# Two attention blocks and two expert layers on one core: last two pairs of batches with banks of their own, three context tiles ahead

## The reference, cut to what matters

```python
x = x + tanh(g_xattn[0]) * L0_xattn(layernorm(x), ctx, ctx)          # 32 batches x 128 rows x 256, 16 heads
x = x + tanh(g_ffn[0])   * L0_ffn(layernorm(x))                      # 8 experts, best 2 per row, width 1024
x = x + tanh(g_xattn[1]) * L1_xattn(layernorm(x), ctx, ctx, bias)    # "second attention"
x = x + tanh(g_ffn[1])   * L1_ffn(layernorm(x))                      # 16 slots read x, one expert each; x reads the slots
```

## Time and profile before

| | |
|---|---|
| median of 3 runs | 1308.04 us (1307.53 to 1308.72) |
| the profiled execution | 1310.88 us |
| its span, first to last instruction | 1309.1 us |
| busy: PE, DVE, ACT, POOL | 1268.9, 881.8, 795.5, 747.3 us |
| mean granted clock of TensorE | 0.996 |
| second attention begins | about 757 us |
| `combine()` begins | about 1240 us |

### The profile page before, as it was taken

One profiled execution on the slowest core, in us unless ns is written; L12 is line 12 of the kernel. 1 busy time (PEld: TensorE's weight loads), 2 busy tenths in 40 slices (PEclk: granted clock), 3 DMA queues, 4 the chain that ended last, 5 costly groups with the idle time before them and its releaser, 6 DMA issues.

```text
span 1309.1 us, 38203 instructions
## 1 busy us (share of the span) xinstructions
PE 1268.9 (97%) x14755; PEld 1133.8 (87%) x14755; DVE 881.8 (67%) x2364; ACT 795.5 (61%) x1739; POOL 747.3 (57%) x835
## 2 busy tenths in 40 slices
PE   9999999998999999999999988999999999999897
PEld 8898888886999999999999967899999998655576
DVE  5888888876566556655564048999999997321386
ACT  5676676654777777777775436665566665423453
POOL 2578888754877787777773054566666643000131
PEclk9999999999999999999999989999999999999999
DMA  6675565633777777777767512621111111599712
GB/s 225 231 257 175 193 207 172 218 131 117 258 221 221 239 216 225 217 231 231 220 213 278 232 45 66 229 93 51 53 51 55 53 61 66 223 428 426 296 64 68
DMA packets 103891, 237.51 MB, mean 181 GB/s; under 512 B 8992, under 2 KB 86176, under 8 KB 91296
## 3 DMA queue, kind: packets, MB, share of 16 engines
q1 hardware_dynamic: 97568, 218.29, 48.7%
q0 software_dynamic: 6144, 16.79, 4.0%
HBM read 174.22 MB, written 60.82 MB: 180 GB/s over the span
## 4 chain that ended last, share of the span: by engine, by line
PE 89%; DVE 4%; DMA 3%; issue 2%; ACT 1%; POOL 1%; DVEq 0%; ACTq 0%; SPq 0%; PEldq 0%; POOLq 0%
PE ps L2140 14%; PE psT L2125 7%; PE ps L714 6%; PE psS L691 5%; PE ps L1084 5%; PE psT L700 4%; PE ps L1026 4%; PE ps L2125 4%; PE psS L2125 4%; PE ps L1009 2%; PE ps L1043 2%; PE ps L953 2%; PE psT L706 2%; DMA arena<-wset_dram 2%; PE ps L2381 2%
## 5 line engine op out<-in xcount | busy, mean ns | idle before, releaser
L2093 POOL TENSOR_TENSOR wb_lo<-arena,wb_hi 128x2048 fp32r<-128x2048 f32 x64 | 296.7, 4637 | 92.0 <-ACT wb_hi L2216 92.0
L2140 PE MATMUL ps<-wb_hi,hT_hi 128*128 128x256 f32 x528 | 151.7, 287 | 0.0
L700 PE MATMUL psT<-arena 32*128 32x128 f32 x2048 | 149.4, 283 | 0.4 <-ACT arena L1256 0.4
L2140 PE MATMUL ps<-wb_lo,hT_hi 128*128 128x256 f32 x528 | 147.7, 280 | 0.0
L2140 PE MATMUL ps<-wb_hi,hT_lo 128*128 128x256 f32 x528 | 147.6, 280 | 0.0
L691 PE MATMUL psS<-arena 32*128 32x256 f32 x1024 | 139.7, 389 | 0.8 <-ACT arena L1333 0.4
L2216 ACT CAST wb_hi<-arena 128x1024 fp32r<-128x1024 f32 x128 | 130.7, 1045 | 4.5 <-DMA arena<-w_dram 4.3
L700 PEld LDWEIGHTS psT<-arena 32*128 32x128 f32 x2048 | 124.6, 186 | 1.7 <-issue 1.2
L1700 POOL TENSOR_TENSOR arena<-arena,eps_sb 128x1 f32<-128x1 f32 x94 | 23.7, 252 | 149.7 <-DVE arena L1571 106.5
L2281 DVE TENSOR_TENSOR arena<-ps,arena 128x512 f32<-128x512 f32 (+1 forms) x39 | 25.4, 651 | 121.5 <-PE ps L2140 81.1
L1713 POOL DMA_INDIRECT arena<-xs_rows,slot_i x64 | 64.4, 1007 | 69.3 <-DMA xs_rows<-arena 54.3
(11 more groups left out here) (508 smaller groups left out, 3862.4 us busy)
## 6 DMA issues: line engine op xcount, KB each, us to landing
arena<-wset_dram SPq DMA_DIRECT2D x24, 2048.0 KB, 16.0
xs_rows<-arena SPq DMA_DIRECT2D x33, 1024.0 KB, 8.8
arena<-w_dram SPq DMA_DIRECT2D x32, 1028.0 KB, 5.9
arena<-w_dram SPq DMA_DIRECT2D x32, 1024.0 KB, 5.9
arena<-w_dram SPq DMA_DIRECT2D x7, 2052.0 KB, 13.3
w_sb<-xs_rows SPq DMA_DIRECT2D x33, 256.0 KB, 2.7
xs_rows<-arena SPq DMA_DIRECT2D x33, 256.0 KB, 5.5
arena<-ctxT_dram SPq DMA_DIRECT2D x63, 128.0 KB, 4.3
```

The source lines that it names most:

```text
L700: nc.tensor.matmul(psT[:, b, j * P:(j + 1) * P], kbd_[p, (k - 1) % NK, c, par, :], qT[p, (k - 1) % 3, c, :], start=j == 0, stop=False, ski ...
L2093: nc.gpsimd.tensor_tensor(wb_lo[:, u % 2, part], wb_raw[:, u % 2, part], wb_hi[:, u % 2, part], ALU.subtract).then_inc(w_g.sem, 1)
L2140: last = nc.tensor.matmul(ps[5][:, t * D:(t + 1) * D], hp[:, f, t * P:(t + 1) * P], wp[:, f, :], start=f == 0 and t == 0 and n == 0, stop= ...
```

## The change

Second attention: `LATE` is 3, so that tile 10 too has its keys and values made at the entry. Its keys come right behind those of tiles 8 and 9, its values in step 0 between the transposition of tile 1 and the second half of the scores of tile 0; the bank is `ps[4]`. The eight constant products at the entry become two, with two more in step -1 and two at the head of step 0; the eight in step 0 become three. The casts of `o1`, `v1` and `dv` move ahead of the early tiles on ScalarE, the one of `dv` behind a wait for the experts' last rows on DVE. GpSimd's subtractions of `o1` and `dv` move ahead of its wait for these rows in DRAM and thus ahead of the first gather; that of `v1` moves to step 1, behind the gather of tile 4. Weight sets 0 to 2 load at steps 5 to 7 as before, set 3 at step 11 instead of 8.

`combine()`: the output products of pair 14 go to `ps[3]` and no longer wait for the residual sum of pair 13. Pair 15 is done by batches: `pn` in two halves, transpositions into `ps[2]` and `ps[5]`, two copies, output products into `ps[4]` and `ps[6]`, two residual sums, and each batch's output DMA waits for its own sum. Three constant products stand in the last step between the transpositions of pair 14 and its output products.

```diff
-LATE = 2
+LATE = 3
...
-        hi_a, lo_g = track("hi_a", "k0 v0 o1 v1 dv", 1), track("lo_g", "k0 v0 o1 v1 dv", 1)
+        hi_a, lo_g = track("hi_a", "k0 v0 o1 v1 dv", 1), track("lo_g", "k0 v0 o1 dv v1", 1)
...
-                    if not A and k == 4 + EARLY_SETS:
+                    if not A and 5 <= k < 4 + EARLY_SETS:
+                        sp.dma_start(set_at(k - 5).rearrange("p e f -> p (e f)"), a["wset"][k - 5]).then_inc(ld_set[k - 5], 16)
+                    if not A and k == ctx_first:
                         sp.wait_ge(kv_a.sem, kv_a.at(ctx_first - 1, "V"))
-                    if not A and 5 <= k < 5 + EARLY_SETS:
-                        sp.dma_start(set_at(k - 5).rearrange("p e f -> p (e f)"), a["wset"][k - 5]).then_inc(ld_set[k - 5], 16)
+                        sp.dma_start(set_at(EARLY_SETS - 1).rearrange("p e f -> p (e f)"), a["wset"][EARLY_SETS - 1])\
+                            .then_inc(ld_set[EARLY_SETS - 1], 16)
...
+                def constant_products(n, bank):
+                    for _ in range(n):
+                        nc.tensor.matmul(ps[bank][:, :], ident_b[:, :], ident_b[:, None, :].to_broadcast([P, 4, P]),
+                                         start=True, stop=True)
...
-                    for _ in range(8):
-                        nc.tensor.matmul(ps[4][:, :], ident_b[:, :], ident_b[:, None, :].to_broadcast([P, 4, P]),
-                                         start=True, stop=True)
+                    for n in range(LATE - 1):
+                        late_keys(n)
+                        late_values(n)
+                    late_keys(LATE - 1)
+                    constant_products(2, 0)
                 for k in steps:
                     if not A and k == 0:
-                        pe.wait_ge(stash_a, STASH + LATE)
+                        constant_products(2, 7)
+                        pe.wait_ge(stash_a, STASH + LATE - 1)
...
+                    if not A and k == -1:
+                        constant_products(2, 0)
+                    if not A and k == 0:
+                        late_values(LATE - 1)
                     scores(k, 1)
...
                     if not A and k == 0:
-                        for _ in range(8):
-                            nc.tensor.matmul(ps[4][:, :], ident_b[:, :], ident_b[:, None, :].to_broadcast([P, 4, P]),
-                                             start=True, stop=True)
+                        constant_products(3, 7)
...
                     nc.scalar.activation(table[:, :], ones[:, 0:1], ACT.Exp)
+                    for name in parts:
+                        if name == "dv":
+                            act.wait_ge(m0_last["y"].sem, m0_last["y"].at(UNITS - 1, "y"))
+                        nc.scalar.copy(split[name][0][:, :, :], w[name]).then_inc(hi_a.sem, 1)
...
-                    for name in parts:
-                        nc.scalar.copy(split[name][0][:, :, :], w[name]).then_inc(hi_a.sem, 1)
+                    for n in range(LATE - 1):
+                        late_away(n)
...
+                    if not A and k == 0:
+                        late_away(LATE - 1)
...
                 if not A:
+                    rest_of("o1")
+                    rest_of("dv")
                     for u in range(2):
                         pool.wait_ge(m0_last["ys"][u], 16 * ((UNITS + 1 - u) // 2))
                     gather(0)
...
+                    if not A and k == 1:
+                        pool.wait_ge(kv_p.sem, kv_p.at(early - 1, "V"))
+                        pool.wait_ge(stash_p, STASH + LATE)
+                        rest_of("v1")
...
+            last_turned, last_out = (ps[2], ps[5]), (ps[4], ps[6])
+
+            def out_bank(i):
+                return ps[3] if i == N - 2 else ps[7]
...
-                    sp.wait_ge(o_v.sem, o_v.at(i, "out"))
                     for b in range(2):
+                        sp.wait_ge(o_v.sem, o_v.at(i, "out") + (b if i == N - 1 else 0))
...
+                def last_pair():
+                    for b in range(2):
+                        pe.wait_ge(p_v.sem, p_v.at(N - 1, "pn") + b)
...
+                    for b in range(2):
+                        pe.wait_ge(t_a.sem, t_a.at(N - 1, "pT") + b)
...
+                    if i == N - 1:
+                        pe.wait_ge(v_a.sem, v_a.at(N // 2 - 1, "v3"))
+                        for _ in range(3):
+                            nc.tensor.matmul(ps[5][:, :], ident_b[:, :], ident_b[:, None, :].to_broadcast([P, 4, P]),
+                                             start=True, stop=True)
...
-                        before(pe, o_v.sem, o_v.at(i - 2, "out"))
+                        if i - 1 < N - 2:
+                            before(pe, o_v.sem, o_v.at(i - 2, "out"))
...
+                        if i == N - 1:
+                            for b in range(2):
+                                nc.vector.tensor_tensor(cpn[:, b].rearrange("p (h s) -> p h s", h=H),
+                                                        e[:, b].rearrange("p (h s) -> p h s", h=H),
+                                                        csm[:, b, :, None].to_broadcast([P, H, NS]), ALU.mult).then_inc(p_v.sem, 1)
```

More of the change, by code:

```diff
@@ L299, in build @@
         stash += [late_rows[:, n * 2 * D:(n + 1) * 2 * D] for n in range(LATE)]
-        late_ctx = [pT[:, 0, n * C * P:(n + 1) * C * P].rearrange("p (c t) -> p c t", c=C) for n in range(LATE)]
-        late_bank = (1, 2)
+        late_ctx = [pT[:, n // 2, n % 2 * C * P:(n % 2 + 1) * C * P].rearrange("p (c t) -> p c t", c=C) for n in range(LATE)]
+        late_bank = (1, 2, 4)
         dead = w_sb[:, 0:8].rearrange("p n c d -> p (n c d)")
@@ L785, in ahead_values, with late_keys, late_values @@
                     last.then_inc(stash_p, 1)
+                def late_keys(n):
+                    pe.wait_ge(ld_stash[n], 32)
+                    for m in range(C):
+                        for c in range(C):
+                            nc.tensor.matmul(ps[late_bank[n]][:, m * P:(m + 1) * P], wk[:, c, m * P:(m + 1) * P],
+                                             late_ctx[n][:, c, :], start=c == 0, stop=c == C - 1)
+                def late_values(n):
+                    for c in range(C):
+                        last = nc.tensor.matmul(ps[late_bank[n]][:, D:2 * D], late_ctx[n][:, c, :], wv[:, c, :],
+                                                start=c == 0, stop=c == C - 1)
+                    last.then_inc(stash_p, 1)
+                def constant_products(n, bank):
+                    for _ in range(n):
+                        nc.tensor.matmul(ps[bank][:, :], ident_b[:, :], ident_b[:, None, :].to_broadcast([P, 4, P]),
+                                         start=True, stop=True)
                 def last_tiles(pe):
@@ L1218, in put_away, with late_away @@
                     nc.scalar.copy(stash[stash_order[n]], ps[stash_bank[n]][:, :]).then_inc(stash_a, 1)
+                def late_away(n):
+                    act.wait_ge(stash_p, STASH + n + 1)
+                    nc.scalar.copy(stash[STASH + n], ps[late_bank[n]][:, :]).then_inc(stash_a, 1)
                 if A:
@@ L1228, in scalar @@
                         values(i, early_bank[i])
-                    for n in range(LATE):
-                        act.wait_ge(stash_p, STASH + n + 1)
-                        nc.scalar.copy(stash[STASH + n], ps[late_bank[n]][:, :]).then_inc(stash_a, 1)
-                    for name in parts:
-                        nc.scalar.copy(split[name][0][:, :, :], w[name]).then_inc(hi_a.sem, 1)
+                    for n in range(LATE - 1):
+                        late_away(n)
                 for k in steps:
@@ L2616, in tensor @@
                 for i in range(N + 1):
+                    if i == N:
+                        last_pair()
+                        break
                     if ok(i - 1):
```

55 lines of the change are left out of this document (36 added, 19 removed).

## The result

| | before | after |
|---|---|---|
| median of 6 runs each | 1308.38 us (1306.98 to 1309.13) | 1300.79 us (1298.48 to 1302.00) |
| ratio | | 0.9937, interval 0.9918 to 0.9955 |
| the profiled execution, its span | 1310.88, 1309.1 us | 1301.76, 1300.0 us |
| experts' last sum to the end of the span | 554.65 us | 543.75 us |

The change makes the kernel 7.6 us faster; forecast were 5.6. In a later and larger measurement (12 runs of the changed kernel, 32 of the one before) it was 5.7 us, ratio 0.9955 (0.9942 to 0.9968). The two intervals overlap.

The account below looks back on a forecast made before the run. TensorE, busy 97% of the span, and its low clock were taken to bound the kernel. Terms 0.75 + 1.4 - 0.1 + 0.5 + 3.1 = 5.65 us off 1308.04 gave 1302.4 us, its own range 1301.2 to 1304.6.

Parts of the forecast that it names:

- Entry: Entry of second attention: line 1072 of tile 0 starts at about 773.35 instead of 777.10, 3.75 us against the profiled execution.
- Most timed runs don't have the first fall: Clock fall at 770.2 us, entry of second attention, worth 3.0 us: taken as absent from most timed runs.
- the 0.75: Gain in us at the entry of second attention in an execution whose clock does not fall there.
- They may well have the second: Clock fall at 1299.3 us, in the last two pairs: timed runs may have it, so 3.1 us was summed there.
- The subtractions: Casts of line 1617 in steps 1 and 2 without GpSimd's subtractions beside them: 0.86 and 0.55, together 1.4 us (0 to 1.7).
- Late first gather: Subtractions of `o1` and `dv` ahead of the first gather make it later: 0.1 us loss, 1.3 as the bad end.
- Tile 10: Stream of tiles: one step less that computes its own keys and values, 0.5 us (0 to 0.6).
- The end: Last two pairs: 3.1 us gain (2.4 to 3.4) against the profiled execution, 1.6 us where the clock does not fall there.
- (b): Gathers, layer norm and GpSimd set the path into tile 1, entry gain is waited away: 1305.4 or 1306.2 us; chance 0.13.
- (d): The change does not do what it says, another wait ends last, entry gives 0.75 or less: 1307.0 us; chance 0.06.
- (a): Timed runs have both clock falls, as the profile has: gain 8.65 us, 1299.4 us; chance 0.20.
- (c): Slower: clock falls and stays down, three constant products being too few; 1311.9 us with 35 us of low clock; chance 0.06.

Follow-up runs that it names:

- before_three: The kernel before with three constant products in step 0 instead of eight, nothing else: 1306.86 us, ratio 0.9994.
- subs_in_steps: The changed kernel with GpSimd's three subtractions back in steps 0, 1 and 2: 1303.28 us, ratio 0.9973.
- before_again: The kernel before once more, unaltered, for a second trace of it: 1306.33 us, ratio 0.9988.
- late_two: The changed kernel with two tiles made early instead of three, constant products in the place of tile 10: 1302.41 us, ratio 0.9965.
- no_fill: The changed kernel without the constant products at the entry, at the head of steps -1 and 0, and in step 0: 1302.69 us, ratio 0.9980.

## Why the prediction was right or wrong

The number, 1302.4, is 1.6 us above the median; the range held it. Forecast rightly was the direction and, term by term against the profiled execution, most of the sum. The step that failed is the reading of the 2.84 us between profile and median: which of the two low stretches the timed runs have. It failed twice, in opposite directions, and the forecast gain of 5.65 us agrees with the 5.7 of the larger measurement by luck.

- **What bounds.** TensorE's own list and its low clock: right.
- **Entry, against the profile shown: 3.75 forecast, 3.94 measured.** Line 1087 comes 16.14 us after the first gather (forecast 16.4, before 20.1) and 3.3 us after the start of the second half's score products; the 3.7 that the prediction gave for this was slipped, its own 773.35 - 770.12 is 3.2. Of the measured gain 1.64 us are the longer low stretch of that one execution, 1.16 the five products less, and 1.08 the subtraction of `o1` (`before_three`, `subs_in_steps`). These three leave 0.06. The last was taken at 0.2, since in the profile it overlapped little of the cast; where it overlaps it costs over 1.
- **"Most timed runs don't have the first fall": wrong.** With it fails the 0.75. All four traces with the old entry have a fall there, and none of 117 executions has a mean clock of 1.0. Between the profile shown and `before_again` it was not the presence of that fall that differed but its length (1.64), and beside it the fall at the end (1.69) and slower steps between tiles 1 and 9 (1.48): the 5.0 us, with 0.2 later on. The median lies between the two, since other executions have low stretches in other places. In the usual execution the entry is worth 21.01 - 18.71 = 2.30 us, where the forecast had 0.75.
- **"They may well have the second": wrong too.** Of the four traces with the old end one, the profile shown, loses time to a fall there; in the three others it takes 9.35 or 9.36 us from the end of pair 14's copy to the end of the span, against 11.03. So the 3.1 in the sum should have been the 1.6 that the prediction kept for the other case. This error of 1.5 us cancels the 1.55 at the entry.
- **The subtractions: 1.4 forecast, 0.85 + 0.54 = 1.39 measured** in the steps behind tile 0 and tile 1, against `before_again`; 0.86 and 0.55 were the terms. The casts of line 1641 of tiles 0 to 2 are at 0.17 us. The price per cast was right, the count was not: a third cast, in step 0, was at stake, and its 1.08 us stand in the entry's gain. `v1` in its new place lengthens nothing: the reduction out of PSUM beside it takes 1.22 us, as others do.
- **Late first gather: 0.1 forecast, 0.03 measured** (2.57 against 2.54 us). The prediction's sign of being wrong, "over 2.5 us", was met before the change already.
- **Tile 10: 0.5 forecast, 0.6 measured** (`late_two`). Set 3's later load costs nothing: the steps around tile 11 are 10.65 and 10.66 us before and after.
- **The end: 3.1 with the fall, measured 3.1; 1.6 without it, measured 1.5.** From the end of pair 14's copy to the end of the last issue it takes 6.06 instead of 9.18 us, and 7.50 in `before_again`; the last issue starts 5.7 us behind that copy, as forecast. But the ground was partly another: I had credited the new bank and the clock, and at full clock the bank is worth 0.25.
- **The sum.** With 2.30 for the entry instead of 0.75, and the end without a fall: 2.30 + 1.39 + 0.6 + 1.5 = 5.8 us; the two traces `before_again` and after differ by 5.9. Timed gains were 7.6, then 5.7.
- **Rivals.** (b) and (d) fall with the entry's gain; (b)'s 1305.4 also leaves out the 0.5 of tile 10 that its own sentence keeps. (a) was half right: the first fall is nearly always there, the second mostly not. Its 1299.4 us is about as far from the median of 1300.79 us as the forecast. (c) did not happen in the changed kernel; in `no_fill` a third of the executions have about what it described, at 1309.5 to 1311.9 us.

The rule of the Trainium skill that the prediction weighed ("TensorE: Matmul & The Clock Gate", "What's actually happening": slow by default, lifted by activity) agrees with `no_fill`, where 4 of 12 executions without the few bf16 products have a mean clock of 0.988 to 0.991. It does not say which gap brings a fall: 1.20 us of waiting passed at 1.00 in the profiled execution of that kernel.

## What to carry to other kernels

Before you subtract two times of one kernel to learn which stalls its usual execution has, look at a second trace: here half of the difference between the profiles was one execution's own. Read an instruction that is many times its median against what the other engines run at that moment, and count it in each step where it can recur, also where it overlaps little in the trace at hand. And where two errors of one sum have opposite signs, a number that comes out right says nothing for either: here 0.75 for 2.30 and 3.1 for 1.5 gave the gain of the larger measurement. A filler that seems idle work can be worth nothing in most executions and 10 us in some, here in 4 of 12.

## What the runs showed of the hardware

- The place and the length of low-clock stretches differ between executions of one program: at the entry 3.4 us (771.5 to 775.0) or 6.8 us (770.2 to 777.1), and at 18, 29, 55 or 297 us in some executions. The median of the kernel before rises from 1304.93 us at a mean clock of 0.999 (10 runs) to 1310.32 at 0.995 (2 runs).
- A cast of 16 columns on VectorE (0.17 us) that meets a subtraction on GpSimd ends 0.03 to 0.05 us after it. It took 0.40 to 1.05 us beside one of 128x512 and 0.63 to 0.65 beside one of 128x256. A reduction of 128x1024 out of PSUM beside one took its usual 1.22 us.
- In the shown execution of the kernel before, the steps from tile 4 to tile 8 took 10.16 to 10.42 us where the three other traces with the old entry have 10.02 to 10.20. What made them longer stays open.
